# Global attentions: diagonal score tiles copied out by ScalarE and masked by GpSimd, and both leading max pieces put behind the first score pair

## The reference

```python
def _L0_attn_ref(x, wq, wk, wv, wo):        # 16 heads of 16, 4 key/value heads, causal
    q = (x @ wq.T).reshape(b, s, NKV, GS, HD)
    k = (x @ wk.T).reshape(b, s, NKV, HD)
    v = (x @ wv.T).reshape(b, s, NKV, HD)
    att = jnp.einsum('bsgmd,btgd->bgmst', q, k) / scale
    att = jnp.where(causal, -jnp.inf, att)
    att = jax.nn.softmax(att, axis=-1)
    ctx = jnp.einsum('bgmst,btgd->bsgmd', att, v).reshape(b, s, DIM)
    return ctx @ wo.T
def _L1_attn_ref(x, wq, w_down, wk_up, wv_up, wo):   # 16 heads of 16, causal by pages of 64
    ...
    pages = jnp.arange(T) // PAGE_SIZE
    allowed = pages[None, :] <= pages[:, None]
    scores = jnp.where(allowed[None, None], scores, jnp.finfo(scores.dtype).min)
    attn = jax.nn.softmax(scores, axis=-1)
    out = jnp.einsum('bhqk,bkhd->bqhd', attn, v).reshape(B, T, E)
```

## Time and profile before

| | |
|---|---|
| time, median of 3 runs | 5498.16 us |
| profiled execution | 5505.85 us, span 5504.3 us |
| PE busy | 4333.2 us (79%) |
| DVE busy | 3117.9 us (57%) |
| ACT busy | 2342.5 us (43%) |
| POOL busy | 1217.9 us (22%) |
| first attention (149.5 to 1107.4) | 957.9 us |
| second attention (2475.0 to 3491.0) | 1016.0 us |

### The profile page before, as it was taken

One profiled execution on the slowest core, in us unless ns is written; L12 is line 12 of the kernel. 1 busy time (PEld: TensorE's weight loads), 2 busy tenths in 40 slices (PEclk: granted clock), 3 DMA queues, 4 the chain that ended last, 5 costly groups with the idle time before them and its releaser, 6 DMA issues. The chain is left out here.

```text
span 5504.3 us, 82496 instructions
## 1 busy us (share of the span) xinstructions
PE 4333.2 (79%) x24804; PEld 2724.9 (50%) x24804; DVE 3117.9 (57%) x6686; ACT 2342.5 (43%) x4143; POOL 1217.9 (22%) x1610
## 2 busy tenths in 40 slices
PE   4899999952989995649989899657796976689687
PEld 2433433341888884324333334345565755566466
DVE  1787777641444442648777777267454437656444
ACT  1365555621444442214555555323454433355333
POOL 1011111015000002110111110123585003378300
PEclk9788878875999997777878776789898988899888
DMA  7211311023112112352223330233453113345211
GB/s 219 33 29 32 48 31 28 11 101 115 57 49 76 47 48 67 118 129 32 40 40 49 49 57 11 90 108 116 150 157 110 31 48 107 120 156 158 69 34 35
DMA packets 327165, 413.82 MB, mean 75 GB/s; under 512 B 40804, under 2 KB 236257, under 8 KB 323260
## 3 DMA queue, kind: packets, MB, share of 16 engines
q1 hardware_dynamic: 278620, 257.43, 14.9%
q0 software_dynamic: 43616, 148.19, 12.7%
q10 hardware_dynamic: 4608, 4.20, 0.2%
HBM read 252.64 MB, written 156.19 MB: 74 GB/s over the span
## 5 line engine op out<-in xcount | busy, mean ns | idle before, releaser
L491 ACT ACTIVATE G_p<-G_psc 128x1024 f32<-128x1024 f32 (+3 forms) x640 | 541.9, 894 | 426.0 <-PE G_psc L454 423.6
L491 ACT ACTIVATE B_p<-B_psc 128x1024 f32<-128x1024 f32 (+3 forms) x640 | 541.7, 894 | 370.7 <-PE B_psc L454 367.9
L515 DVE TENSOR_REDUCE G_mpart<-G_pm 128x1 f32<-128x512 f32 x768 | 485.2, 684 | 150.0 <-PE G_pm L416 148.2
L416 PE MATMUL G_pm<-G_ks,G_qs 48*128 48x512 f32 (+3 forms) x1280 | 491.2, 521 | 89.3 <-DMA G_ks<-G_one 58.7
L515 DVE TENSOR_REDUCE B_mpart<-B_pm 128x1 f32<-128x512 f32 x768 | 483.8, 684 | 98.6 <-PE B_pm L416 96.5
L416 PE MATMUL B_pm<-B_ks,B_qs 48*128 48x512 f32 (+3 forms) x1280 | 480.1, 506 | 74.5 <-DMA B_ks<-B_one 42.9
L1705 POOL TENSOR_SCALAR J_pr<-J_pr,J_rc 128x256 f32<-128x256 f32 x512 | 462.7, 915 | 41.2 <-DVE J_rc L1843 38.8
L416 PEld LDWEIGHTS G_pm<-G_ks,G_qs 48*128 48x128 f32 x1280 | 229.9, 227 | 478.4 <-DVE G_mpart L515 222.9
L416 PEld LDWEIGHTS B_pm<-B_ks,B_qs 48*128 48x128 f32 x1280 | 222.8, 218 | 450.4 <-DVE B_mpart L515 223.6
L431 PE MATMUL G_po<-G_p,G_v 128*32 128x512 f32 (+3 forms) x2560 | 371.2, 657 | 20.5 <-DVE G_o L528 18.9
L431 PE MATMUL B_po<-B_p,B_v 128*32 128x512 f32 (+3 forms) x2560 | 353.3, 628 | 21.9 <-DVE B_o L528 19.3
(11 more groups left out here) (307 smaller groups left out, 7962.1 us busy)
## 6 DMA issues: line engine op xcount, KB each, us to landing
J_v<-lve SPq DMA_DIRECT2D x64, 520.0 KB, 3.8
J_k<-lkT SPq DMA_DIRECT2D x64, 512.0 KB
lve<-I_v SPq DMA_DIRECT2D x64, 260.0 KB, 2.1
lqT<-I_tT SPq DMA_DIRECT2D x64, 256.0 KB, 2.4
lkT<-I_tT SPq DMA_DIRECT2D x64, 256.0 KB, 2.6
J_q<-lqT SPq DMA_DIRECT2D x64, 256.0 KB
ein<-Z_z SPq DMA_DIRECT2D x8, 1228.0 KB
E_xin<-ein POOLq DMA_DIRECT2D x8, 1152.0 KB, 6.3
```

Of the source, the lines that this page charges most:

```text
L416: last = pe.matmul(t[:, n * w:(n + 1) * w], qs[s][rows, qb // SUB, h // 2, qb % SUB * P:(qb % SUB + 1) * P], ks[s][rows, h // 2 % NA, kc * ...
L491: act.activation(p[:, t % 2, 2 * pr:2 * pr + 2, off:CH], psc[:, 2 * pr:2 * pr + 2, off:CH], ACT.Exp, scale=SC).then_inc(e_done[pr], 1)
L515: dve.tensor_reduce(mpart[:, heads[0] % 2, heads[0] // 2, qb, kc:kc + 1], pm[slots[e]][:, 0:w], AX, ALU.max).then_inc(max_done, 1)
```

## The change

Six edits, all in `attention`:

1. The diagonal 128x128 tiles leave the pieces. A new event, `diag`, computes four of them (two heads, two query blocks) with four matmuls of 128 columns into one bank; there are 16 in an iteration. Pieces end before the diagonal; there are 128.
2. ScalarE copies a `diag` bank to SBUF (`dm`, four slots), GpSimd masks it there (an affine select in the first attention, a memset in the second), and VectorE reduces it six events later.
3. VectorE's custom masked maximum, its accumulator reads, the mask tile `far` and its input are gone.
4. ScalarE, not VectorE, copies `po` to `o`.
5. Both leading events of a window stand behind the first score pair; none stands behind the second. Turns and `diag`s are sorted to the end of their window.
6. The list's last entry takes bank 1 when the first one would follow in its own bank.

```diff
+        if qb % 2 == 0:
+            off = [("diag", (qb, 0))] + off[:2] + [("diag", (qb, 1))] + off[2:]
...
+        held = [x for x in held if x[0] == "piece"] + [x for x in held if x[0] != "piece"]
...
+    slots = [e % RING for e in range(NE)]
+    if NE % RING == 1:
+        slots[-1] = 1
...
@@ gpsimd
+            def cut_diagonal(k, e, clears):
...
+                wait_apart(pool, d_out, k * ND + d + 1, fence)
+                tile = dm[:, d % DSLOTS]
+                if page == 1:
+                    pool.affine_select(out=tile, in_=tile, pattern=[[0, 2 * PAR], [-1, P]], compare_op=ALU.is_ge,
+                                       fill=-3e38, base=0, channel_multiplier=1).then_inc(d_cut, 1)
+                else:
+                    for q in range(page, P, page):
+                        last = pool.memset(tile[q - page:q, :, q:P], -3e38)
+                    last.then_inc(d_cut, 1)
@@ tensor
+                if kind == "diag":
+                    qb, u = what
+                    parts = [(h, q, q * P, P) for h in (u, u + 2) for q in (qb, qb + 1)]
+                else:
+                    qb, kc, w, heads = what
+                    parts = [(h, qb, kc * CH, w) for h in heads]
...
                         score.then_inc(s_done, 1)
-                        some(pr, pr + 1)
+                        if pr == 0:
+                            some(0, 2)
@@ scalar
+                if kind == "diag":
+                    d = number[e]
+                    act.wait_ge(s_max, k * NI + issued[e] + 2)
+                    if not static(k, 0) or d >= DSLOTS:
+                        act.wait_ge(d_max, k * ND + d + 2 - DSLOTS)
+                    act.activation(dm[:, d % DSLOTS], pm[slots[e]][:].rearrange("p (n k) -> p n k", k=P), ACT.Copy
+                                   ).then_inc(d_out, 1)
...
+                act.activation(o[:, qc % 2], po[:], ACT.Copy).then_inc(o_done, 1)
@@ vector
-                    if diag:
-                        for x, head in enumerate(heads):
-                            last = dve.tensor_tensor_reduce(pm[slots[e]][:, x * w:(x + 1) * w], pm[slots[e]][:, x * w:(x + 1) * w], far[:, CH - w:CH],
-                                                            1.0, -3e38, ALU.add, ALU.max,
-                                                            mpart[:, head % 2, head // 2, qb, kc:kc + 1])
+                        dve.wait_ge(d_cut, (k - back) * ND + d + 2)
+                        dve.tensor_reduce(mpart[:, u, :, qb:qb + 2, NC4],
+                                          dm[:, d % DSLOTS].rearrange("p (a q) k -> p a q k", q=2), AX, ALU.max
+                                          ).then_inc(d_max, 1)
```

More of the change, by code:

```diff
@@ L220, in spread @@
-    def spread(i, t):
-        return [(i + e // NE, e % NE) for e in range(cut[t], cut[t + 1]) if exists(i + e // NE, e % NE)]
-    opening = [(0, e) for e in range(cut[0]) if exists(0, e)]
+    order, close = [], {}
+    for qb in range(NQ):
+        off = []
+        for kc in range(qb // SUB):
+            off += [("piece", (qb, kc, CH, [h])) for h in range(GRP)]
+        rest = qb % SUB * P
+        if rest > CH // 2:
+            off += [("piece", (qb, qb // SUB, rest, [h])) for h in range(GRP)]
+        elif rest:
+            off += [("piece", (qb, qb // SUB, rest, [u, u + 2])) for u in range(2)]
+        if qb % 2 == 0:
+            off = [("diag", (qb, 0))] + off[:2] + [("diag", (qb, 1))] + off[2:]
+        order += off
+        close[qb // SUB] = len(order) - 1
@@ new lines, in attention @@
+    NE = len(order) + NC4
+    late_of = {}
+    for c in reversed(range(NC4)):
+        at = close[c] + TURN_BEHIND
+        late_of[c] = int(at >= len(order))
+        order.insert(at % len(order), ("turn", c))
+    cut = [NE * (t + AHEAD) // NS for t in range(NS + 1)]
+    ring = [None] * NE
+    for t in range(NS):
+        held = [order[e % NE] for e in range(cut[t], cut[t + 1])]
+        held = [x for x in held if x[0] == "piece"] + [x for x in held if x[0] != "piece"]
+        for x, e in zip(held, range(cut[t], cut[t + 1])):
+            ring[e % NE] = x
@@ new lines, in attention @@
+    late = [late_of[x[1]] if x[0] == "turn" else 0 for x in ring]
+    number, count = [], {"piece": 0, "diag": 0, "turn": 0}
+    for kind, what in ring:
+        number.append(what if kind == "turn" else count[kind])
+        count[kind] += 1
+    NP, ND = count["piece"], count["diag"]
+    issued = [sum(x[0] != "turn" for x in ring[:e]) for e in range(NE)]
+    NI = NP + ND
+    slots = [e % RING for e in range(NE)]
+    if NE % RING == 1:
+        slots[-1] = 1
+    after = [[] for _ in range(NE)]
@@ new lines, in attention @@
+    last_of = {c: (0, 0, 0) for c in range(NC4)}
+    for e, (kind, what) in enumerate(ring):
+        if kind == "diag":
+            after[(e + REDUCE_BEHIND) % NE].append(("reduce", e, (e + REDUCE_BEHIND) // NE))
+        if kind != "turn":
+            c = what[0] // SUB
+            ready_at, pieces_done, diags_done = last_of[c]
+            if kind == "piece":
+                last_of[c] = (max(ready_at, e), number[e] + 1, diags_done)
+            else:
+                last_of[c] = (max(ready_at, e + REDUCE_BEHIND), pieces_done, number[e] + 1)
@@ L226, in attention, with exists, window @@
+    for c in range(NC4):
+        e = last_of[c][0] + 1
+        after[e % NE].append(("fold", c, e // NE))
+    def exists(k, back):
+        return not isinstance(k, int) or 0 <= k - back < NIT
+    def window(i, t):
+        return [(i + e // NE, e % NE) for e in range(cut[t], cut[t + 1])]
+    opening = [(0, e) for e in range(cut[0])]
     with ExitStack() as ctx:
@@ L438, in body @@
                     off = max(0, kb - SUB * qc) * P
-                    events = [(e // NE, e % NE) for e in range(cut[t], cut[t + 1]) if exists(i + e // NE, e % NE)]
                     if kb == 0:
@@ L443, in some @@
                     def some(a, z):
[L444 to L446 removed]
+                        for x in range(cut[t] + a, min(cut[t] + z, cut[t + 1])):
+                            nxt, e = x // NE, x % NE
+                            if nxt and e == 0 and exists(i + 1, 0):
                                 pe.wait_ge(q_in[1 - s], half * (16 * LOADS) + 16 * LOADS)
@@ L461, in body @@
                         weigh(i - 1, 1 - s, NS - 1)
-                    some(2, len(events))
+                    some(2, NE)
             pe.wait_ge(c_in, 16 * CONSTS)
@@ L534, in _ @@
-            dve.tensor_copy(far[:, CH - P:CH], mqk[:]).then_inc(far_set, 1)
-            dve.wait_ge(far_set, 3)
+                kind, what = ring[e]
+                if kind == "piece" and exists(k, 0):
+                    qb, kc, w, heads = what
+                    a, z = heads[0] // 2, heads[-1] // 2 + 1
+                    dve.wait_ge(s_max, k * NI + issued[e] + 2)
+                    dve.tensor_reduce(mpart[:, heads[0] % 2, a:z, qb, kc],
+                                      pm[slots[e]][:, 0:len(heads) * w].rearrange("p (h k) -> p h k", k=w),
+                                      AX, ALU.max).then_inc(max_done, 1)
```

200 lines of the change are left out of this document (85 added, 115 removed).

## The result

The changed kernel takes 5627.08 us, the median of 4 runs (5609.36 to 5695.38). The kernel before took 5492.51 us in the same comparison (4 runs). The ratio is 1.0231, with a 95% interval of 1.0192 to 1.0270: slower by 2.3%, where 5335 us was forecast. The profiled execution took 5623.05 us, with a span of 5621.5 us.

What follows compares the result with a forecast made beforehand. TensorE was taken as the bound, with waits for VectorE and clock falls. Waits -60, pairing with diagonal tiles -60, ScalarE +20, row of maxima -20, clock -45 gave -165 us from 5505.85, less 7.7: 5335 us, range 5260 to 5455.

Steps and rivals of the forecast that it cites:

- The rival on the slower side: ScalarE becomes the bound in full steps with a `diag`, its copies landing on the path; 5560 us, chance 0.07.
- Leading pieces side by side: Each step's two leading pieces, issued together, cost 0.34 us instead of 0.53 apart: 0.2 less a step, 119 us in all.
- Waits removed: TensorE's waits for the `po` copy, the list-start bank and the custom maximum: 60 of 89.6 us taken back.
- Diagonal tiles on TensorE: Four narrow matmuls of a `diag` in one half of the array, less narrower pieces: +60 us in both attentions.
- VectorE: Relieved by 4 to 13 us an iteration, no term of its own; lets full-clock steps fall below 2.71 us.
- ScalarE: Gets the `diag` and output copies, 190 us in both attentions, mostly fitting its idle time; cost +20 us.
- GpSimd: Gets 16 masks an iteration, needed by VectorE only six events later; cost 0, bounds 0 and +15 us.
- The row of maxima: Second attention: its DMA, issued a step earlier, takes 20 off TensorE's 31.9 us wait.
- The clock: Removing a quarter of the falls to half clock gives about 3 us an iteration, 45 us in 15 iterations.
- the rival of moved waits: TensorE waits for ScalarE's `diag` copies where it waited for VectorE, and the clock stays; 5430 us, chance 0.2.

Runs made afterwards that it cites:

- experiment 1: Changed kernel with one leading piece behind each score pair again, all its other edits kept; 5355.16 us, ratio 0.9775 to the kernel before.
- experiment 2: Kernel before the change, with only the order edit: both leading pieces behind the first score pair; 5760.92 us, ratio 1.0484.
- experiment 3: Changed kernel with both leading pieces behind the second score pair instead of the first; 5371.83 us, ratio 0.9782 to the kernel before.
- experiment 9: Kernel before the change, with only two edits: the list's last entry in bank 1, and `po` copied out by ScalarE; 5358.52 us, ratio 0.9789.
- Experiment 5: Changed kernel, VectorE reducing only the first 128 columns of each piece (other maxima left out); 5192.27 us, ratio 0.9436 to the kernel before.
- experiment 8: Changed kernel with one piece behind each score pair, the third ahead of `weigh`, only the fourth behind it; 5480.63 us, ratio 0.9971 to the kernel before.
- experiment 6: Kernel before the change, with only the bank of the list's last entry changed; 5432.73 us, ratio 0.9861.
- experiment 7: Kernel before the change, with only the copy of `po` moved from VectorE to ScalarE; 5414.34 us, ratio 0.9834.

## Why the prediction was wrong

The forecast was 5335 with a range of 5260 to 5455; 5627 lies outside, on the other side of the kernel before, to which the prediction gave 0.07. The rival on the slower side was ScalarE, and it was not ScalarE either.

**The step that failed is "Leading pieces side by side".** It priced two pieces issued together from the trailing pair, 0.34 us, and took 119 us off for it. The trailing pair starts together because both banks are long free. The leading b takes the bank of c, which is free 1.28 us after c was issued, and the front text says itself that a piece waits for the reduction of the piece three before it. What follows is that b's earliest start is fixed by VectorE, wherever b stands in the list. Put ahead of the second score pair it gains nothing and holds that pair up. The rows were there: 640.65 (c) to 641.93 (b) is 1.28 us. The step was read as filled with work, when in it the score pair was covering a wait. The term was forecast at -119 (net -60 with the diagonal matmuls) and turned out as +272 by experiment 1 and +271 by experiment 2 for the order alone (some 250 and 266 by the ratios).

Part of the 272 is direct. A step of four events whose second piece waits is 0.24 us longer at full clock (2.94 against 2.70) or 0.42 at half (4.59 against 4.17), and diagonal steps lengthen by up to 0.24 as well. Twelve of an iteration's 40 windows have only three events (148 is 28 x 4 + 12 x 3), and a full step of that kind is no longer (405.52 to 407.64, 2.12 us; experiment 1 has 2.10). Experiment 1 and the changed kernel differ by 151 us in the first attention. An estimate, from each step of the changed kernel's trace against the same step of experiments 1 and 3 at the same granted clock: some 60 to 75 us of it are longer steps, and 75 to 90 that the clock goes from 0.88 to 0.75. It is an estimate because the others have few steps at half clock, and the missing ones were scaled. Both come from the order, which is all that experiments 1 and 2 change; what in the longer steps brings the clock down stays open.

**Waits removed** (forecast 60 us of 89.6): as forecast, but visible only in experiment 1. There the pieces wait 9.8 us for VectorE in the first attention, where the kernel before has 45.5 with the copy, and nothing waits for the copy. In the changed kernel, copy waits went and b's wait came in: 57.4 us (28.3 + 29.1) are there again. The wait at the list's start has not gone there; it is 0.70 us instead of 1.41:

```profile
480.61 0.44 PE L470 MATMUL B_pm<-B_ks,B_qs 48*128 48x128 f32 x2 [0.70 <-DVE B_mpart L580]
```

**Diagonal tiles on TensorE** (forecast +60): too dear. In the step behind the one shown, the four narrow matmuls stand between score matmuls of 384 columns (left out here):

```profile
456.60 0.22 PE L470 MATMUL B_pm<-B_ks,B_qs 48*128 48x128 f32 x1
...
456.83 0.33 PE L470 MATMUL B_pm<-B_ks,B_qs 48*128 48x128 f32 x2
457.01 0.38 PE L507 MATMUL B_psc<-B_qs,B_ks 50*128 50x384 f32 x1
```

They start within 0.3 us of each other, and from the first of them to the next score matmul it is 0.41 us, not the 0.54 that was taken. Experiments 1 and 9 put them, with all that they save, at about zero.

**VectorE** was forecast below 90 us an iteration and is at 86. That it would let a full step fall below 2.71 was wrong: the step is not set by VectorE's four reductions (2.48) but by the bank's round, which holds only one of them. Experiment 5 is the only kernel whose full steps with four pieces are shorter, and it is the only one that shortens that reduction.

**ScalarE** (forecast +20) and **GpSimd** (0): no loss seen. A diagonal copy takes 598 ns for an estimated 595, and in experiment 1 only 2.1 us of the pieces' waiting is for ScalarE.

**The row of maxima** (forecast -20): the wait in the second attention went from 31.9 to 28.2 us, and is 32.0 in experiment 1. In one iteration of the changed kernel (SP, then TensorE), against the earlier trace rows:

```profile
2867.97 1.30 SPq L406 DMA_DIRECT2D G_qs<-G_mrow  x2
```
```profile
2892.54 0.80 PE L507 MATMUL G_psc<-G_qs,G_ks 50*128 50x512 f32 x2 [5.59 <-DMA G_qs<-G_mrow]
```

A small DMA still takes 24.6 us from issue to use. It is issued a step earlier, but the loads are issued in that very step. The Trainium skill (DMA: Bandwidth & Descriptors, Queues, rings and completion order) has an engine go round robin between queues, by which the move gives nothing. The total agrees with that, and the 24.6 us do not, so the agreement may be by chance.

**The clock** was right in kind. With the waits gone and the order kept, it rose from 0.82 to 0.88 in the first attention, and the gain was over what was forecast: without the pairing term the sum would have been 119 us higher, 5452, and experiment 1 measured 5355. For the change as made it had the wrong sign: steps that are longer, with a gap in each at full clock, went with a clock of 0.75.

In the rival of moved waits one sum is off: -60 from 5498 is 5438, not 5430. Nothing hangs on it.

## What to carry to other kernels

Before an instruction of an in-order engine is moved forward, work out the earliest time at which its buffer is free (issue of the last user, its duration, the reader's duration, the hand-over), and compare it with the new place. If it is later, the move only turns covered time into a wait for all that stands behind it. With few buffers in a ring, a step has a lower bound that no busy share shows: here 1.28 us from the last user to the next, plus what stands behind it until that user comes again.

## What the runs showed of the hardware

- From the issue of a 128x512 piece to the start of the next one in its bank it takes 1.28 us at full clock: 0.54 to the start of the reduction (453.38 to 453.92), 0.68 for the reduction, and 0.06 for the hand-over (what is left). It is 1.28 in the kernel before, the changed one and experiments 1 and 8. At half clock it is 1.58 (568.50 to 570.08): only the part ahead of the reduction is longer, 0.83.
- Waits of about 0.3 us in the full steps are little in the view of waits (28.3 us in the first attention, of which 9.8 are in experiment 1 too), but they go with 151 us in time. At half clock the same order costs 0.42 us a step and no wait is recorded at all; only the timeline shows it.
- In experiments 6 and 7, removing 17 and 38 us of TensorE's waits gave 64 and 83 us, each with the granted clock up from 0.841 to 0.856.
